# The third sweep (second batch norm's output, third layer norm) and the edge attention as one list of slots instead of loops one after the other

## Chip, cores and metric

The kernel runs on one core of a Trainium2 chip. The metric is the time of one execution on the device in microseconds (us); the median of three runs is given. TensorE multiplies matrices, VectorE (DVE in the rows) and ScalarE (ACT) work element by element, GpSimd (POOL) does so more slowly, and SyncE (SP) issues the transfers.

## The reference

`x` has 16 batches of 512 nodes with 128 features. Four graph blocks follow one another, each with a residual and a layer norm. The change touches the end of the third block and the whole fourth:

```
x = _layernorm(x + _L2_gnn_ref(x, adj, ...), axis=-1)      # out = batchnorm(out, g2, be2), added to x
x = _layernorm(x + _L3_gnn_ref(x, ..., adj, src, dst), axis=-1)
# _L3: 256 edges src -> dst, 4 heads of 32 features
Xq, Xv = H @ W_lin.T, H @ W_val.T
e  = einsum(leaky_relu(Xq[src] + Xq[dst], 0.2), a) + log(A0[src, dst] + EPS)
attn = softmax of e over the edges that share a src           # segment_max, exp, segment_sum
Y  = segment_sum(attn * Xv[dst], src);  return Y @ W_out.T
```

The second batch norm needs statistics over all 16 batches before it can be applied to any. After it, no batch depends on another.

## The kernel before

All of `X` stays in SBUF. The first 880 us compute the first two blocks and the graph product of the third; the change leaves their instructions and order alone. Then `phase_batchnorm` runs three sweeps over the batches. The second (L1864) multiplies by W2 and gathers statistics. Then `batch_norm` makes scale and shift (last write at L1935). The **third** sweep takes, per batch, the scaled output (`z`, ScalarE, L1894), its four transposes (L1875), the residual add (L1961) and four row statistics (L606) on VectorE. Per quad of four batches GpSimd makes layer-norm scale and shift (`norm_scales`, thirteen instructions L571 to L586, among them the inverse root L583), and ScalarE and VectorE apply them (L646, L625).

`phase_attention` begins when all engines have left that block. It has two loops. The **gather** loop splits X into a high and a low part (`aXH` on ScalarE, `aXL` on GpSimd, L72), multiplies both by the incidence matrix `GZ` (L2337, eight matmuls a batch), copies the result to `Z` (L2262), projects to scores and values (L2343, L2346, copied to `aUV` at L2146), takes the leaky ReLU `lr` (L2270) and the head scores (L2355). The softmax is done by scans along the sorted edges (L2237 to L2251), for three quads at once beside the last gather quad, and for the fourth after it. The attention weights `aT` of all batches are made in one go (L2292, L2293). Only then the **attend** loop starts: GpSimd weights the values (`va`, L2107), ScalarE and VectorE split them (`vah`, `val`), TensorE scatters them (L2386) and projects (L2376), VectorE adds (L2304) and takes statistics, GpSimd makes the norm of a quad, ScalarE applies it, SyncE stores.

Each engine runs its own list in order. A semaphore wait on an engine holds all that stands behind it. The loops are hardware loops (`Fori`) with their first and last pass written out (`peeled`). PSUM has eight banks of 128x512; in the gather loop banks 0 and 1 hold the gathered batch, 2 and 3 the projections, 4 the scores.

Of the kernel before, what the change touches and what calls it, by code (L numbers as in the profile page):

```python
# [552 lines left out]
SHIFT_LINKS = 6  # L553


def norm_scales(pool, sh, n, stats, work, mean, rstd, own, before, shift, free=None):

    a, b, c = (work[:, k, 0:n] for k in range(3))

    def const(k):
        return sh.const[:, k, 0:n]

    def link(k, ins):

        ins.then_inc(own, 1)
        pool.wait_ge(own, before + k)

    pool.tensor_tensor(a, stats[:, :, 1], stats[:, :, 4], ALU.add)  # L571
    pool.tensor_tensor(b, stats[:, :, 1], stats[:, :, 4], ALU.subtract)
    link(1, pool.tensor_tensor(c, stats[:, :, 2], stats[:, :, 5], ALU.add))
    pool.tensor_tensor(mean, a, const(sh.HALF), ALU.mult)
    pool.tensor_tensor(c, c, const(sh.PER_D), ALU.mult)
    link(2, pool.tensor_tensor(b, b, b, ALU.mult))
    link(3, pool.tensor_tensor(b, b, const(sh.QUARTER), ALU.mult))
    link(4, pool.tensor_tensor(b, b, c, ALU.add))
    link(5, pool.tensor_tensor(b, b, const(sh.EPS), ALU.add))
    if free is None:  # L580
        free = lambda: None
    pool.tensor_tensor(mean, mean, const(sh.MINUS), ALU.mult)
    link(6, pool.tensor_tensor(a, b, const(sh.ROOT), ALU.pow))  # L583
    free()
    pool.tensor_tensor(rstd, a, const(sh.ONE), ALU.mult)
    return pool.tensor_tensor(shift, mean, a, ALU.mult)  # L586


class NormBuffers:
# [3 lines left out]
    def __init__(self, sb, sem, sh):  # L593
        self.sh = sh
        self.rows = QB * sh.C
        self.stats = sb("nstats", [P, sh.NB * sh.C, 6])
        self.work = sb("nwork", [P, 3, self.rows])
        self.mean = sb("nmean", [P, self.rows])
        self.scale = sb("nscale", [P, self.rows])
        self.shift = sb("nshift", [P, self.rows])  # L600
        self.own = sem("norm_own")
        self.ready = sem("norm_ready")
# [10 lines left out]
    def scales(self, pool, g, own, before, free=None):  # L613

        return norm_scales(pool, self.sh, self.rows, self.stats[:, bass.ds(self.rows * g, self.rows), :],
                           self.work, self.mean[:, :], self.scale[:, :], own, before, self.shift[:, :], free)

    def apply_on_dve(self, dve, n, b, chunks=None, other=None):

        scale, shift = other or (self.scale, self.shift)  # L620
        C = self.sh.C
        for c in range(C) if chunks is None else chunks:
            k = b * C + c
            row = self.sh.X[:, c, bass.ds(n, 1), :]
            ins = dve.tensor_scalar(row, row, scale[:, k:k + 1], shift[:, k:k + 1], ALU.mult, ALU.add)  # L625
        return ins

    def finish_scales(self, pool, earlier):
        self.scales(pool, self.sh.NB // QB - 1, self.own, SHIFT_LINKS * earlier).then_inc(self.ready, 1)

    def finish(self, act, earlier, done, batches=range(QB)):
        act.wait_ge(self.ready, earlier + 1)
        for b in batches:
            self.apply(act, self.sh.NB - QB + b, b).then_inc(done, 1)

    def apply(self, act, n, b, chunks=None, other=None):

        scale, shift = other or (self.scale, self.shift)
        C = self.sh.C
        for c in range(C) if chunks is None else chunks:
            k = b * C + c
            row = self.sh.X[:, c, bass.ds(n, 1), :]
            ins = act.activation(row, row, ACT.Identity, bias=shift[:, k:k + 1], scale=scale[:, k:k + 1])  # L646
# [3 lines left out]
def take_over(nc, sh, later):  # L650
# [36 lines left out]
    sh.free_to = first  # L687
    sh.hidden = room("hidden", [P, NB, J, N], offset=first)
# [1134 lines left out]
def phase_batchnorm(nc, sh, d):  # L1823
# [8 lines left out]
    with ExitStack() as ctx:  # L1832
# [5 lines left out]
        O2 = nc.alloc_sbuf_tensor_at("O2", [P, NB, N], F32, offset=sh.outputs_at)  # L1838
        tmp = sh.A
        st2 = sb("st2", [P, 1, NB, 6])  # L1840
        bmv = sb("bmv", [P, J + 1, 2])
        bsc = sb("bsc", [P, J + 1])
        bsh = sb("bsh", [P, J + 1])
        norm = sh.norm
        names = ("own", "bmv_done", "bve", "brstd", "bn_done", "u_done", "o_mm", "o_out",
                 "ost_done", "z_done", "z_mm", "z_add", "stat_done", "norm_own", "rstd_done", "x_done", "xd_done")
# [3 lines left out]
        def xb(b):  # L1850
            return sh.X[:, :, bass.ds(b, 1), :].rearrange("p c o d -> p c (o d)")

        def by_chunk(ap):
            return ap.rearrange("p (c d) -> p c d", c=C)

        @block.tensor
        def _(pe):
# [10 lines left out]
            def third(i, last):  # L1868
                for b in range(QB):
                    n = QB * i + b  # L1870
                    pe.wait_ge(S["z_done"], n + 1)
                    wait(pe, S["z_add"], n - QB + 1)
                    for c in range(C):
                        cols = slice(c * P, (c + 1) * P)
                        ins = pe.transpose(sh.psum[:, b, cols], tmp[:, b, cols], sh.ident[:, :])  # L1875
                    ins.then_inc(S["z_mm"], 1)

            peeled(pe, NQ, second)
            peeled(pe, NQ, third)

        @block.scalar
        def _(act):
# [9 lines left out]
            def z(n, b):  # L1892
                wait(act, S["z_mm"], n - QB + 1)
                act.activation(tmp[:, b, :], O2[:, bass.ds(n, 1), :], ACT.Identity,  # L1894
                               bias=bsh[:, J:J + 1], scale=bsc[:, J:J + 1]).then_inc(S["z_done"], 1)

            def third(i, last):

                for b in range(QB):
                    if not last:  # L1900
                        z(QB * (i + 1) + b, b)
                    if not isinstance(i, int) or i > 0:
                        if b == 0:
                            act.wait_ge(S["rstd_done"], i)
                        norm.apply(act, QB * (i - 1) + b, b, range(C - 1)).then_inc(S["x_done"], 1)

            act.wait_ge(S["bn_done"], 1)
            peeled(act, NQ, second)
            act.wait_ge(S["bn_done"], 2)
            for b in range(QB):  # L1910
                z(b, b)
            peeled(act, NQ, third)

        @block.vector
        def _(dve):
# [37 lines left out]
            def third_stats(n):  # L1953
                dve.wait_ge(S["z_add"], n + 1)
                norm.take_stats(dve, n).then_inc(S["stat_done"], 1)

            def third(i, last):
                for b in range(QB):
                    n = QB * i + b
                    dve.wait_ge(S["z_mm"], n + 1)  # L1960
                    dve.tensor_tensor(xb(n), by_chunk(sh.psum[:, b, :]), xb(n), ALU.add).then_inc(S["z_add"], 1)  # L1961
                    if not isinstance(i, int) or n >= 1:
                        third_stats(n - 1)
                if not isinstance(i, int) or i > 0:
                    dve.wait_ge(S["rstd_done"], i)
                    for b in range(QB):
# [498 lines left out]
```

## Time and profile before

| | before |
|---|---|
| median of three runs | 1098.01 us (1094.91 to 1099.32) |
| the profiled execution | 1097.92 us, span 1096.1 us |
| third sweep | 921.0 to 957.5 us of the span |
| gather loop | 957.5 to 1030.5 us |
| softmax of the last quad, attention weights | 1030.5 to 1039.3 us |
| attend loop | 1039.3 to 1082.5 us |
| last norms and stores | 1082.5 to 1096.1 us |

The span is what the rows are timed in; the 1.8 us between it and the execution's own time lie outside the rows. A busy share says how long an engine had an instruction in work, not that it set the pace. A short idle time "<-" another engine says whose result ended the wait.

### The profile page before, as it was taken

How to read it: one execution, taken by the hardware profiler on the slowest of the kernel's cores; microseconds unless marked ns; L12 is line 12 of the kernel's file. 1: busy time of each engine (PE TensorE's matmuls, PEld its weight loads, DVE VectorE, ACT ScalarE, POOL GpSimd, SP SyncE). 2: the span in 40 equal slices, each digit the busy share in tenths (PEclk: the TensorE clock that was granted, in tenths of full speed). 3: DMA queues.
4: the chain of work that ended last, by engine and by line, in shares of the span. 5: the costliest groups of instructions: out<-in, count | busy, mean ns of one | idle time of the engine just before them, and what ended most of it. 6: DMA issues, size and time to landing. Idle time of an engine off the chain costs nothing. (4 is left out here: it accounts for less than half of the span.)

```text
span 1096.1 us, 14843 instructions
## 1 busy us (share of the span) xinstructions
PE 957.0 (87%) x5168; PEld 815.9 (74%) x5168; DVE 660.3 (60%) x1528; ACT 547.5 (50%) x1133; POOL 314.6 (29%) x373
## 2 busy tenths in 40 slices
PE   4999998899998999999999999799899886289583
PEld 2677997688997888998789889697689734166463
DVE  4843435334656736666655664788878857643665
ACT  2113233455645554554655554567677474742256
POOL 0001131222232223332223332324332300552256
PEclk9989999999999999999999999999999988589797
DMA  7003001000110000101010101210100000000004
GB/s 206 1 1 76 20 39 70 8 20 1 39 40 1 8 33 19 40 1 39 1 39 20 39 1 42 73 39 21 39 20 1 0 1 1 1 0 1 0 20 134
DMA packets 34137, 31.60 MB, mean 29 GB/s; under 512 B 8594, under 2 KB 28178, under 8 KB 34068
## 3 DMA queue, kind: packets, MB, share of 16 engines
q1 hardware_dynamic: 33108, 30.64, 9.1%
q8 instruction: 40, 0.66, 0.2%
q14 instruction: 29, 0.24, 0.1%
q10 hardware_dynamic: 960, 0.07, 0.1%
HBM read 22.83 MB, written 7.87 MB: 28 GB/s over the span
## 5 line engine op out<-in xcount | busy, mean ns | idle before, releaser
L1371 ACT ACTIVATE gates<-psum,gbias 128x256 f32<-128x256 f32 (+2 forms) x312 | 158.3, 565 | 56.3 <-PE psum L67 52.6
L65 PE MATMUL psum<-LS,WI 128*128 128x256 f32 (+2 forms) x312 | 104.8, 336 | 15.3 <-ACT gates L1371 11.6
L72 POOL TENSOR_TENSOR LS<-A,LS 128x512 fp32r<-128x512 f32 (+2 forms) x44 | 48.7, 1107 | 201.6 <-ACT LS L1356 201.6
L67 PE MATMUL psum<-LS,WI 128*128 128x256 f32 (+2 forms) x312 | 103.4, 331 | 0.0
L66 PE MATMUL psum<-LS,WI 128*128 128x256 f32 (+2 forms) x312 | 103.3, 331 | 0.0
L72 POOL TENSOR_TENSOR LS<-Hodd,LS 128x512 fp32r<-128x512 f32 (+2 forms) x44 | 48.7, 1107 | 160.2 <-ACT LS L1356 160.2
L65 PEld LDWEIGHTS psum<-LS,WI 128*128 128x128 f32 x312 | 60.0, 192 | 26.7 <-POOL LS L72 11.5
L65 PE MATMUL psum<-B2h,LT2h 128*128 128x256 f32 x256 | 72.8, 284 | 1.1 <-DVE X L1479 1.0
L72 DVE TENSOR_TENSOR yl<-psum,yh 128x512 fp32r<-128x512 f32 x58 | 39.7, 689 | 56.4 <-ACT yh L1313 41.4
L1378 ACT ACTIVATE tc<-cell 128x512 f32<-128x512 f32 (+2 forms) x88 | 45.2, 514 | 55.7 <-DVE cell L1659 39.9
L67 PE MATMUL psum<-B2h,LT2l 128*128 128x256 f32 x256 | 72.4, 283 | 0.0
L66 PE MATMUL psum<-B2l,LT2h 128*128 128x256 f32 x256 | 72.4, 283 | 0.0
L65 PE MATMUL psum<-Eh,yh 128*128 128x384 f32 x168 | 59.1, 352 | 12.0 <-DVE yl L72 12.0
L66 PEld LDWEIGHTS psum<-LS,WI 128*128 128x128 f32 x312 | 60.0, 192 | 5.1
L67 PEld LDWEIGHTS psum<-LS,WI 128*128 128x128 f32 x312 | 59.9, 192 | 4.2
L72 POOL TENSOR_TENSOR XSl<-X,XSh 128x512 fp32r<-128x512 f32 x32 | 42.6, 1333 | 69.5 <-ACT XSh L1308 69.3
L65 PE MATMUL psum<-LS,WH 128*128 128x256 f32 (+2 forms) x192 | 60.1, 313 | 0.0
L66 PE MATMUL psum<-LS,WH 128*128 128x256 f32 (+2 forms) x192 | 59.9, 312 | 0.0
L67 PE MATMUL psum<-LS,WH 128*128 128x256 f32 (+2 forms) x192 | 59.9, 312 | 0.0
L66 PE MATMUL psum<-El,yh 128*128 128x384 f32 x168 | 58.0, 345 | 0.0
L67 PE MATMUL psum<-Eh,yl 128*128 128x384 f32 x168 | 58.0, 345 | 0.0
L606 DVE BATCH_NORM_STATS2 nstats<-X 128x6 f32<-128x128 f32 (+1 forms) x256 | 55.1, 280 | 1.6 <-DVE X L2304 1.3
(388 smaller groups left out, 2718.5 us busy)
## 6 DMA issues: line engine op xcount, KB each, us to landing
WI<-lstm_weights SPq DMA_DIRECT2D x14, 512.0 KB, 3.5
WH<-lstm_weights SPq DMA_DIRECT2D x11, 512.0 KB, 4.5
X<-in_x SPq DMA_DIRECT2D x16, 256.0 KB, 5.0
out<-X SPq DMA_DIRECT2D x32, 128.0 KB, 1.9
lstm_weights<-WI SPq DMA_DIRECT2D x4, 512.0 KB, 2.6
lstm_weights<-WH SPq DMA_DIRECT2D x3, 512.0 KB, 2.6
A<-in_adj SPq DMA_DIRECT2D x1, 1024.0 KB, 6.2
z_A<-in_adj SPq DMA_DIRECT2D x1, 1024.0 KB, 5.1
```

The costliest lines, as they stand in the source:

```text
L65: pe.matmul(out, lhs[0], rhs[0], start=start, stop=False)
L66: pe.matmul(out, lhs[0], rhs[1], start=False, stop=False)
L67: return pe.matmul(out, lhs[1], rhs[0], start=False, stop=stop)
L72: return eng.tensor_tensor(out, full, high.bitcast(F32), ALU.subtract)
L606: return dve.bn_stats(self.stats[:, bass.ds(self.sh.C * n + c, 1), :], self.sh.X[:, c, bass.ds(n, 1), :])
L1371: act.activation(gates[:, gate, 0:n], sh.psum[:, gate, 0:n], ACT.Tanh if gate == G else ACT.Sigmoid, bias=gbias[:, p_ - 1, gate:gate + 1]) ...
L1378: act.activation(tcs[:, 0:n], cell[:, s % 2, 0:n], ACT.Tanh).then_inc(S["tanh_done"], 1)
```

## The change

The third sweep leaves `phase_batchnorm` and joins `phase_attention`. There every batch passes through all steps in a software pipeline, written as one flat list `order` that every engine walks through without a loop, taking its own items. Slot k holds, for different batches, these items: `z` and `T` (transpose, residual add) of batch k+5, `s3`/`v3`/`p3`/`sh3`/`ap3` (row statistics, variance, inverse root, shift and application of the third norm, in groups of one or two batches), `xs` (split) of batch k+2, `G` (gather) of batch k, `U` of k-1, `lr` and `W` of k-2, and from slot 9 on `S` (scatter) of batch k-9, `P` (projection) of k-10, and `R` (residual add), `s4` and the fourth norm of k-11 and older. The softmax of quad g stands in slots 4g+6 and 4g+7 (`sc`, `mx`, `df`, `ex`, `su`, `at`), so batches 0 to 3 can be attended to from slot 7.

The arithmetic of a norm moves: six short VectorE instructions and a shift replace twelve of the thirteen on GpSimd, which keeps the inverse root. `Z` is copied from PSUM by ScalarE instead of VectorE. The applications of the third norm are split 2+2, 1+3 or 3+1 chunks between VectorE and ScalarE by batch (`chunks3`), those of the fourth 2+2. The low part of the weighted values (`vl`) of batches 0 to 7 goes to GpSimd, of 8 to 15 to VectorE. PSUM: banks 0, 1 and 6 rotate among what VectorE reads (`T`, `at`, `P`), 2 to 5 among what ScalarE reads (`G`, `U`, `S`), 7 holds scores. The edge constants are made once instead of four times, in `phase_batchnorm` right behind the first `batch_norm`. The output goes out in 16 transfers of 256 KB, not 32 of 128 KB.

```diff
...
+    AHEAD, BEHIND = 5, 9
...
+        GROUPS3 = [(0, 1), (1, 2), (2, 3)] + [(b, min(b + 2, NB)) for b in range(3, NB, 2)]
+        GROUPS4 = [(0, 4), (4, 8), (8, 12), (12, 14), (14, 16)]
+        def first_part():
+            return [("z", 0), ("z", 1), ("T", 0), ("z", 2), ("s3", 0), ("v3", 0), ("p3", 0), ("T", 1), ("z", 3), ("s3", 1),
+                    ("v3", 1), ("p3", 1), ("T", 2), ("z", 4), ("sh3", 0), ("ap3", 0), ("xs", 0), ("s3", 2), ("v3", 2),
+                    ("sh3", 1), ("ap3", 1), ("xs", 1), ("p3", 2), ("T", 3), ("s3", 3)]
+        def slot(k):
+            t, m = k + AHEAD, k - BEHIND
+            g, part = divmod(k - 6, QB)
+            softmax = part if 0 <= g < NQ else None
+            ready = [i for i, (b0, b1) in enumerate(GROUPS3) if b1 == t and k > 1] + [2] * (k == 0) + [3] * (k == 1)
+            items = [("p3", i) for i in ready if i > 2]
+            if 0 <= m + 1 < NB:
+                items += [("vh", m + 1)]
+            if k == 0:
+                items += [("z", t)]
+            if t + 1 < NB:
+                items += [("z", t + 1)]
+            if 0 <= k - 2 < NB:
+                items += [("lr", k - 2)]
+            if softmax == 0:
+                items += [("sc", g), ("mx", g), ("df", g)]
+            if 0 <= m - 2 < NB:
+                items += [("R", m - 2)]
+            if 0 <= m + 1 < NB:
+                items += [("vl", m + 1)]
+            if 0 <= m - 2 < NB:
+                items += [("s4", m - 2)] + [("v4", i) for i, (b0, b1) in enumerate(GROUPS4) if b1 == m - 1]
+            if k < NB:
+                items += [("G", k)]
+            if k == 0:
+                items += [("T", t - 1)]
+            if t < NB:
+                items += [("T", t)]
+            if 4 <= k + 2 < NB:
+                items += [("xs", k + 2)]
+            if softmax == 0:
+                items += [("ex", g)]
+            if 0 <= k - 1 < NB:
+                items += [("U", k - 1)]
+            if softmax == 1:
+                items += [("at", g)]
+            items += [("sh3", i) for i in ready]
+            items += [("ap3", n) for n in ((2,), (3, 4))[k] if n < NB] if k < 2 else [("ap3", k + 3)] * (k + 3 < NB)
+            if k < 2:
+                items += [("xs", k + 2)]
+            if k == 0:
+                items += [("s3", t - 1), ("v3", 3)]
+            if t < NB:
+                items += [("s3", t)] + [("v3", i) for i, (b0, b1) in enumerate(GROUPS3) if b1 == t + 1]
+            if softmax == 0:
+                items += [("su", g)]
+            if 0 <= m < NB:
+                items += [("S", m)]
+            if 0 <= k - 2 < NB:
+                items += [("W", k - 2)]
+            if 0 <= m - 1 < NB:
+                items += [("P", m - 1)]
+            if 0 <= m + 2 < NB:
+                items += [("va", m + 2)]
+            items += [("p4", i) for i, (b0, b1) in enumerate(GROUPS4) if b1 == m - 1]
+            for i, (b0, b1) in enumerate(GROUPS4):
+                if b1 == m - 2:
+                    items += [("sh4", i)]
+                if b0 <= m - 2 - (b1 - b0) < b1:
+                    items += [("ap4", m - 2 - (b1 - b0))]
+            return items
+        order = first_part()
+        for k_ in range(NB + BEHIND + 5):
+            order += slot(k_)
+        for g_, (b0_, b1_) in enumerate(GROUPS4):
+            order += [item for item in [("sh4", g_)] + [("ap4", b) for b in range(b0_, b1_)] if item not in order]
...
+        def chunks3(n):
+            split = C // 2 if n < 3 else C - 1 if 5 < n < 11 else 1
+            return range(0, split), range(split, C)
+        def low_on_dve(n):
+            return n >= NB - BEHIND + 1
+        dve_ring, act_ring = {}, {}
+        for item_ in order:
+            if item_[0] in ("T", "at", "P"):
+                dve_ring[item_] = len(dve_ring)
+            elif item_[0] in ("G", "U", "S"):
+                act_ring[item_] = len(act_ring)
+        DVE_BANKS, ACT_BANKS = (0, 1, 6), (2, 3, 4, 5)
+        def dve_bank(item):
+            return sh.psum[:, DVE_BANKS[dve_ring[item] % len(DVE_BANKS)], :]
+        def act_bank(item):
+            return sh.psum[:, ACT_BANKS[act_ring[item] % len(ACT_BANKS)], :]
...
+            def variances(rows, work):
+                stats = norm.stats[:, rows, :]
+                a, b, c = (work[:, k, rows] for k in range(3))
+                dve.tensor_tensor(a, stats[:, :, 1], stats[:, :, 4], ALU.add)
+                dve.tensor_tensor(c, stats[:, :, 2], stats[:, :, 5], ALU.add)
+                link(dve.tensor_tensor(b, stats[:, :, 1], stats[:, :, 4], ALU.subtract))
+                link(dve.scalar_tensor_tensor(b, b, 0.25, b, ALU.mult, ALU.mult))
+                link(dve.scalar_tensor_tensor(b, c, 1.0 / D, b, ALU.mult, ALU.add))
+                return dve.tensor_scalar(b, b, EPS, None, ALU.add)
...
+            def roots(k, groups, g):
+                work, scale, _ = norms[k - 3]
+                rows = slice(C * groups[g][0], C * groups[g][1])
+                pool.wait_ge(S[f"var{k}"], g + 1)
+                pool.tensor_tensor(scale[:, rows], work[:, 1, rows], sh.const[:, sh.ROOT, 0:rows.stop - rows.start],
+                                   ALU.pow).then_inc(S[f"root{k}"], 1)
...
```

What TensorE had in its gather loop, the end of one pass (two batches: the last two of sixteen gather matmuls, the two batches' projections, their scores):

```order
L2337 MATMUL psum<-z_GZ,aXH 128x512
L2337 MATMUL psum<-z_GZ,aXL 128x512
L2343 MATMUL psum<-Z,z_aWT 128x256
L2346 MATMUL psum<-z_aWT,Z 128x128 x2
L2343 MATMUL psum<-Z,z_aWT 128x256
L2346 MATMUL psum<-z_aWT,Z 128x128 x2
L2355 MATMUL psum<-lr,wide 16x256 x2
```

TensorE in slot 10 of the change, from the end of `G` of batch 10 on (`T` of 15, `U` of 9, `S` of 1, `W` of 8, `P` of 0):

```order
L2097 MATMUL psum<-z_GZ,aXH 128x512
L2097 MATMUL psum<-z_GZ,aXL 128x512
L2088 MATMUL psum<-ident,A 128x128 x4
L2105 MATMUL psum<-aZ,z_aWT 128x256
L2108 MATMUL psum<-z_aWT,aZ 128x128 x2
L2136 MATMUL psum<-z_GsT,vah 128x512
L2136 MATMUL psum<-z_GsT,val 128x512
L2136 MATMUL psum<-z_GsT,vah 128x512
L2136 MATMUL psum<-z_GsT,val 128x512
L2116 MATMUL psum<-lr,wide 16x256
L2145 MATMUL psum<-z_aWT,aY 128x128 x4
```

The projections now follow the gather of another batch, and transposes and scatters that stood in loops of their own lie between them and the scores.

VectorE in the last gather pass before, with the softmax of three quads (768 wide) in it:

```order
L2262 COPY Z<-psum 128x512 x2
L2237 SCALAR_TENSOR_TENSOR s<-pf,sco 16x768
L2240 SCALAR_TENSOR_TENSOR s<-pr,s 16x768
L2270 SCALAR_TENSOR_TENSOR lr<-aUV 128x256 x2
L2244 TENSOR_TENSOR s<-sco,s 16x768
L2262 COPY Z<-psum 128x512 x2
L2248 SCALAR_TENSOR_TENSOR s<-kf,s 16x768
L2270 SCALAR_TENSOR_TENSOR lr<-aUV 128x256 x2
L2251 SCALAR_TENSOR_TENSOR sco<-pr,s 16x768
L2277 TENSOR_TENSOR sco<-psum,lg 16x256
```

VectorE in slot 6 of the change, with the softmax of the first quad, up to the `lr` of slot 7:

```order
L2320 TENSOR_TENSOR sco<-psum,lg 16x256
L2275 SCALAR_TENSOR_TENSOR s<-pf,sco 16x256
L2276 SCALAR_TENSOR_TENSOR s<-pr,s 16x256
L2324 TENSOR_TENSOR s<-sco,s 16x256
L2240 TENSOR_TENSOR X<-psum,X 128x4x128
L2263 SCALAR_TENSOR_TENSOR n3shift<-n3work,n3scale 128x8
L2295 TENSOR_SCALAR X<-X,n3scale,n3shift 128x128 x3
L566 BN_STATS nstats<-X 128x6 x4
L2280 SCALAR_TENSOR_TENSOR s<-kf,s 16x256
L2281 SCALAR_TENSOR_TENSOR sco<-pr,s 16x256
L2271 SCALAR_TENSOR_TENSOR lr<-aUV 128x256
```

Two copies to `Z` a pass are gone from this engine; the residual add, the application and the row statistics of the third norm have come in between the scans of one quad.

## Rows read from the trace of the kernel before

**Rows 1.** The profile page, its first line.

```profile
span 1096.1 us, 14843 instructions
```

**Rows 2.** Stages: busy us of PE, PEld, DVE, ACT, POOL; PEclk; DMA share, GB/s.

```profile
921.00:957.50 36.50, 14.32 (x64) 10.84 (x64) 26.16 (x92) 25.44 (x53) 16.04 (x40) 0.59 0.00 0
957.50:1030.50 73.00, 61.06 (x257) 43.93 (x257) 32.84 (x60) 27.81 (x50) 28.27 (x30) 0.91 0.00 1
1030.50:1039.30 8.80, 2.05 (x17) 1.63 (x16) 6.24 (x10) 1.08 (x3) 1.75 (x5) 0.56 0.00 0
1039.30:1082.50 43.20, 35.40 (x192) 29.16 (x192) 30.80 (x95) 27.04 (x67) 28.59 (x73) 0.93 0.17 50
1082.50:1096.10 13.60, 0.00 (x0) 0.00 (x0) 3.59 (x14) 6.70 (x18) 6.97 (x21) 0.51 0.55 154
```

**Rows 3.** Timeline of VectorE, third sweep: start, us, instructions, idle time before them.

```profile
922.96 1.47 DVE L1961 TENSOR_TENSOR X<-psum,X 128x512 f32<-128x512 f32 x2 [2.13 <-PE psum L1875]
...
925.12 0.67 DVE L1961 TENSOR_TENSOR X<-psum,X 128x512 f32<-128x512 f32 x1
925.72 0.86 DVE L606 BATCH_NORM_STATS2 nstats<-X 128x6 f32<-128x128 f32 x4
...
952.48 1.11 DVE L625 TENSOR_SCALAR X<-X,nscale,nshift 128x128 f32<-128x128 f32 x4
```

**Rows 4.** Chain that ended last, a gather pass: start, us, what.

```profile
987.06 3.92 PE psum L2337 x16
990.98 0.43 PE psum L2343 x2
991.41 0.45 PE psum L2346 x4
...
1002.10 0.60 PE psum L2355 x2
```

**Rows 5.** The same chain in the attend loop.

```profile
1048.15 1.19 PE psum L2386 x4
1049.34 0.91 PE psum L2376 x8
```

**Rows 6.** Timeline of TensorE, third sweep: one batch's transposes.

```profile
927.31 0.63 PE L1875 MATMUL psum<-ident,A 128*128 128x128 f32 x4 [0.34 <-ACT A L1894]
```

**Rows 7.** Timeline of VectorE, softmax of the last quad.

```profile
1034.95 0.68 DVE L2251 TENSOR_TENSOR_SCAN sco<-pr,s 16x256 f32<-16x256 f32 x1
1036.19 0.96 DVE L2292 RECIPROCAL inverse<-psum 128x128 f32<-128x128 f32 x1 [0.56 <-PE psum L2366]
```

**Rows 8.** Timeline of an earlier norm, its arithmetic on VectorE, root on GpSimd.

```profile
689.31 0.17 DVE L1508 TENSOR_TENSOR n1work<-nstats 128x8 f32<-128x8 f32 x1
...
690.17 0.68 DVE L1546 TENSOR_TENSOR B<-psum,RB 128x512 f32<-128x512 f32 x1
690.34 1.64 POOL L1774 TENSOR_TENSOR n1scale<-n1work,const 128x8 f32<-128x8 f32 x1 [3.83 <-DVE n1work L1513]
```

**Rows 9.** VectorE beside GpSimd in the gather loop: timelines of both.

```profile
984.92 0.75 DVE L2270 SCALAR_TENSOR_TENSOR lr<-aUV 128x256 f32 x1 [1.03 <-ACT aUV L2146]
...
984.12 1.27 POOL L72 TENSOR_TENSOR aXL<-X,aXH 128x512 fp32r<-128x512 f32 x1 [0.57 <-ACT aXH L2134]
```

**Rows 10.** One line's or tile's instructions: ns of one, min/median/max.

```profile
L2270 DVE SCALAR_TENSOR_TENSOR lr<-aUV x16: 417/426/1536, 967.0 to 1029.4; 128x256 f32<-128x256 f32 x8, 128x256 f32 x8
L625 DVE TENSOR_SCALAR X<-X,nscale,nshift x76: 331/340/1039, 449.4 to 953.3; 128x128 f32<-128x128 f32 x68, - x8
```

**Rows 11.** Groups of instructions by line: busy us, mean ns of one, idle before.

```profile
L72 DVE TENSOR_TENSOR LS<-gates,LS 128x256 fp32r<-128x256 f32 x24 | 22.4, 932 | 0.8
```

**Rows 12.** Attend loop: timelines of GpSimd and VectorE at one root.

```profile
1057.27 2.90 POOL L583 TENSOR_TENSOR nwork<-nwork,const 128x16 f32<-128x16 f32 x1
...
1058.90 0.41 DVE L72 TENSOR_TENSOR val<-va,vah 128x256 fp32r<-128x256 f32 x1
```

**Rows 13.** Timeline of ScalarE, the last norm's application.

```profile
1090.50 1.65 ACT L646 ACTIVATE X<-X,last_shift,last_scale 128x128 f32<-128x128 f32 x4 [2.95 <-POOL last_shift L586]
```

More of the change, by code:

```diff
@@ L550, in _ @@
             done(ins)
[L553 to L586, printed above, removed]
 class NormBuffers:
@@ L625, in apply_on_dve @@
             ins = dve.tensor_scalar(row, row, scale[:, k:k + 1], shift[:, k:k + 1], ALU.mult, ALU.add)
[L626 to L646, printed above, removed]
         return ins
@@ L687, in take_over @@
     sh.free_to = first
+    sh.consts_at = first - 4096
     sh.hidden = room("hidden", [P, NB, J, N], offset=first)
@@ L1951, in second, with edge_constants @@
                         second_stats(n - 1)
[L1953 to L1966, printed above, removed]
-                        ins = norm.apply_on_dve(dve, QB * (i - 1) + b, b, range(C - 1, C))
-                    ins.then_inc(S["xd_done"], 1)
+            def edge_constants():
+                dve.wait_ge(S["wide0"], 1)
+                dve.wait_ge(S["acol_in"], 16)
+                for h in range(NH):
+                    rows = slice(h * DH, (h + 1) * DH)
+                    dve.tensor_copy(wide[rows, R - NH + h:R - NH + h + 1], acol[rows, 0:1])
+                link(dve.tensor_tensor(ne[:, 1:NE], ss[0:R, 0, 1:NE], ss[0:R, 0, 0:NE - 1], ALU.not_equal))
+                dve.tensor_scalar(pf[:, 1:NE], ne[:, 1:NE], LOWEST, None, ALU.mult)
+                dve.tensor_scalar(kf[:, 1:NE], ne[:, 1:NE], -1.0, 1.0, ALU.mult, ALU.add)
+                dve.tensor_scalar(pr[:, 0:NE - 1], ne[:, 1:NE], LOWEST, None, ALU.mult)
+                dve.memset(pf[:, 0:1], LOWEST)
+                dve.memset(kf[:, 0:1], 0.0)
+                dve.memset(pr[:, NE - 1:NE], LOWEST)
             batch_norm(list(range(J)), 0)
+            edge_constants()
             peeled(dve, NQ, second)
@@ L2186, in _, with normalized @@
[L2186 to L2192 removed]
+            def normalized(n):
+                wait(act, S["pe_dve"], dve_ring["T", n - QB] + 1 if n >= QB else 0)
+                act.activation(tmp[:, n % QB, :], O2[:, n, :], ACT.Identity, bias=sh.bsh[:, sh.J:sh.J + 1],
+                               scale=sh.bsc[:, sh.J:sh.J + 1]).then_inc(S["z_done"], 1)
@@ L2275, in scores @@
-            def scores(g):
-                dve.wait_ge(S["sc_mm"], QB * g + QB)
-                dve.tensor_tensor(sco[:, bass.ds(g, 1), :].rearrange("p o e -> p (o e)"), sh.psum[0:R, 4, 0:NE],
-                                  lg[:, :], ALU.add).then_inc(S["sc_done"], 1)
-            def gather_quad(g, last):
-                for h in (0, 1):
-                    wait(dve, S["sc_mm"], QB * g + 2 * h)
-                    gather(g, h, last)
-                scores(g)
-            peeled(dve, NQ, gather_quad)
@@ L2310, in attend @@
-            def attend(i, last):
-                for b in range(QB):
-                    n = QB * i + b
-                    first = isinstance(i, int) and i == 0
-                    weighted_low(n, b)
-                    if not first or b >= 3:
-                        residual(n - 3, (b - 3) % QB)
-                        out_stats(n - 3)
-            peeled(dve, NQ, attend)
-            for n in range(NB - 3, NB):
-                residual(n, n % QB)
-                out_stats(n)
-            for n, made in ((NB - QB, NQ), (NB - QB + 1, NQ), (NB - 1, NQ + 1)):
-                dve.wait_ge(S["rstd_done"], made)
-                norm.apply_on_dve(dve, n, n % QB, other=last_norm).then_inc(S["xd_done"], 1)
@@ new lines, in rows_of, with shifts, leaky @@
+            def rows_of(groups, g):
+                return slice(C * groups[g][0], C * groups[g][1])
+            def shifts(k, g, rows):
+                work, scale, shift = norms[k - 3]
+                dve.wait_ge(S[f"root{k}"], g + 1)
+                dve.scalar_tensor_tensor(shift[:, rows], work[:, 0, rows], -0.5, scale[:, rows], ALU.mult, ALU.mult)\
+                    .then_inc(S[f"shift{k}"], 1)
+            def leaky(n):
+                dve.wait_ge(S["act_free"], act_ring["U", n] + 1)
+                if n >= QB:
+                    dve.wait_ge(S["sc_mm"], n - QB + 1)
+                u = UV[:, n, 0:NE]
+                dve.scalar_tensor_tensor(lr[:, n % QB, :], u, 0.2, u, ALU.mult, ALU.max).then_inc(S["lr_done"], 1)
```

600 lines of the change are left out of this document (281 added, 319 removed).

## Prediction

> **What bounds the kernel now.** The page gives the span, 1096.1 us [rows 1]. I read the part behind the second batch norm stage by stage, since the share of the whole says nothing of it. From 921.0 to the end it lasts 175.1 us in five stages [rows 2]. The reader is to see that no engine is full in any but one of them. In the third sweep TensorE is busy 14.3 of 36.5 us at 0.59 of its clock, VectorE 26.2, and both wait for the norm's scales from GpSimd. In the gather loop TensorE is the bound, 61.1 of 73.0 us, and VectorE has 40 us to spare. The softmax of the last quad and the weights of all batches are a bare chain, 8.8 us. In the attend loop TensorE (35.4) and VectorE (30.8) share 43.2 us. The last 13.6 us are one norm after another on GpSimd, then the stores. Summed over the five rows TensorE has 112.8 us of work (part of it at the low clock) and VectorE 99.6. So a perfect overlap could save at most some 60 us, and what it does save depends on which engine is longest in each stretch of the new list.
>
> **The sum.** I go through the list by stretches and take in each the engine with most work, at durations of the old trace.
>
> *Start.* The first residual add began at 922.96 [rows 3]. The list has a block change ahead of it, which cost some 0.3: 923.3.
>
> *To the end of slot 10, by VectorE.* Sixteen residual adds at 0.60 from start to start and sixteen statistics of four at 0.86 [rows 3]: 23.4. Ten groups of variance, six instructions from 689.31 to 690.17, 0.86, and one shift at 0.17 [rows 8]: 10.3, with the waits in them 10.5. Of the third norm 27 chunks are applied here by then, 1.11 for four [rows 3]: 7.6. Nine `lr` at 0.43 [rows 10]: 3.9. Two quads of softmax: four scans at 0.7 [rows 7] and two 256-wide passes at 0.41 [rows 12] are 3.6 each; weights of the first quad 0.6 (the reciprocal is 0.96 for 128 columns [rows 7] and 32 are left, so between 0.24 and 0.96 with the product; I take the middle). Sum 53.2. TensorE has in the same slots eleven gathers at 1.96, ten projections at 0.88, nine scores at 0.6 [rows 4], twelve transposes at 0.63 [rows 6], two scatters at 1.19 and a projection at 0.91 [rows 5]: 46.7. It cannot begin before batch 0 has been added, normed, applied and split, some 8 us after 923.3; with 3.5 for the low clock (below) that ends at 981.5. So VectorE sets the end, narrowly: 923.3 + 53.2 = 976.5.
>
> *What VectorE waits for in there.* First, crossings: in slot 6 and slot 10 it has some 7.5 us of work where TensorE has 4 to 6, and the weights `at` need the scans done on VectorE, then TensorE, then VectorE again. What stands behind the waiting `at` is the shift and application of the third norm, for which `xs` and `G` of two slots later wait; the two slots of lead cover it. I take 3 us, bounds 0 and 8 (half a slot each time). Second, GpSimd beside it. `lr` started at 984.92 and took 0.75, while `aXL` ran on GpSimd from 984.12 to 985.39; alone it takes 0.42 [rows 9, 10]. It ended 0.28 after the GpSimd instruction, as if it had waited for it. Over sixteen `lr` the median is 0.426 and the longest 1.536 [rows 10], and for the applications 0.340 and 1.039. The row nearest at the upper end is the earlier `LS` subtraction of the same 256 columns, mean 0.932 [rows 11]: half a microsecond of waiting in each. I take 4 us in all, since the median `lr` waits for nothing; bounds 0 and 22 (43 exposed instructions or groups at 0.51). End of slot 10: 983.5.
>
> The Trainium skill, page "SBUF — State Buffer", section "Who interferes with whom", has for this that a VectorE instruction with two SBUF inputs and a GpSimd instruction that reads SBUF exclude each other for the whole instruction. The trace agrees at `lr`, and does not at the inverse root: `val`, two SBUF inputs, took 0.41 at 1058.90 in the middle of a root that ran from 1057.27 to 1060.17 [rows 12]. By the page the roots, moved beside the whole list, would count as blockers too; by the row they don't. What full blocking would give is the rival below.
>
> *Slots 11 to 15, by TensorE.* Gather 1.96, projection 0.88, scores 0.6, scatter 1.19, projection 0.91, so 5.55 a slot, and 0.4 twice for the weights: 28.5, to 1012.0. VectorE has some 20 us here, so it is hidden and can catch up what it lags. `Z` on ScalarE instead of VectorE is hidden as well: ScalarE's list holds about 3.6 us a slot in the first stretch and no more here; if that cover were gone it would cost 0.6 a slot.
>
> *Slots 16 to 25, by VectorE again.* Ten adds with statistics at 1.46 and ten times two chunks of the fourth norm at 0.28: 20.2. Eight `val` at 0.41: 3.3. Two `lr`: 0.9. Three groups' variances: 3.2. The last quad's softmax and weights: 4.2. Sum 31.8, to 1043.8. TensorE has only scatter and projection here, 2.1 a slot against 3.2, and the 2.9 of a four-batch root runs on GpSimd beside it.
>
> *Tail.* Last add and statistics 1.46, variance 0.86, root of eight columns 1.64 and shift 0.17 [rows 8], two batches applied by halves on two engines, on ScalarE 1.65 for four chunks [rows 13], and from the last application to the end what it is today, 1096.1 less 1092.15 [rows 1, 13]: 3.95. Together 9.7, to 1053.5. The last store is one of 256 KB instead of four of 128 KB for two batches; I count no difference, at most tenths.
>
> *Handoffs.* The new list changes partner more often than the loops did, but has no loop registers to count. Bounds 0 and 10 over 30 slots; I take 2.8. End of span 1056.3.
>
> Against its own 1096.1 that is 39.8 less, and with the 1.8 us that the profiled execution has outside its span, 1058.1. The profiled execution (1097.92) and the median (1098.01) are the same, so **1058** is the forecast, 0.964 of before. Edge constants cost nothing: VectorE makes them while the first, slow-clock products of the second sweep run.
>
> **Where the 40 us come from.** The third sweep's 36.5 us mostly go, as its work now lies beside gathers; the bare 8.8 goes; of the attend loop and tail 56.8 become 41.5; the gather stretch stays about as long. It does not shrink, because VectorE and TensorE are near each other there.
>
> **Rivals.**
>
> *Low clock.* TensorE's granted clock was 0.91 over the gather loop and 0.59 and 0.56 in the stages where it mostly idled [rows 2]. 0.91 over 73 us are some 13 us at 1.2 GHz instead of 2.4, which cost about 6.6; I took half. In slots 16 to 25 TensorE is busy 2.1 of 3.2 us. The attend loop kept 0.93 at 35.4 of 43.2 busy, so I expect the high level; if it fell, 4.2 a slot would pass VectorE's 3.2 and cost 10, another 7 us early on 3.5: 1072. Chance 0.12.
>
> *Port waits at mid height.* If the scans, variances and applications all meet `aXL` and the new `vl` on GpSimd, 22 instead of 4 in the first eleven slots, less what slots 11 to 15 absorb: 1066 to 1084. Chance 0.13.
>
> *Port waits all along: slower than before.* GpSimd now has 3.7 us in each of slots 7 to 13, where the gather loop had 1.3 a batch. VectorE has some 135 exposed pieces (16 `lr`, 20 passes of softmax, 8 `val`, 30 variances and shifts, 61 calls of application). At the 0.51 of the `LS` row that is 69 us, 65 more than I count, 8 of them hidden in the middle: 1115. It decides at 0.32 each (44 us). Against it: the median `lr` and the median application show nothing. Chance 0.04.
>
> *No change.* The slots do not overlap: every slot lasts as long as the fullest, 5.55 by 26 slots, and 18 us of start and tail make 162 of today's 175; with waits in the softmax slots 1086 to 1098. For it speaks only that each engine's list is in order. Chance 0.04.
>
> *Better.* No port waits, no crossings, no handoffs: 9.8 less, and 2 or 3 from weights and low clock, 1046. Chance 0.12.
>
> **How the numbers follow.** The forecast, 1050 to 1067, has 0.55. The range 1046 to 1076 takes in the better case, the low clock and the lower half of the port waits. A measurement tells about 0.5% (5.5 us) from no change. Faster by more than that has all of the forecast, better, low clock and middle port cases and half of the no-change case: 0.94. Within it 0.02, slower 0.04.
>
> **What would show it.** Right: the stretch behind the second batch norm is about 135 us; TensorE's clock stays above 0.9 in it after the first 20 us; the first scatter starts near 975, while gathers go on; VectorE is over 90% busy in slots 0 to 10 and TensorE over 90% in 11 to 15; 10 us lie between the last projection's add and the end; ScalarE loads its exponential table once. Wrong: `lr`, scans or applications with means twice their least; long idle times of TensorE "<- DVE lr" in the softmax slots; GpSimd near full, so that `aXL` comes late; the clock at 0.5 in the last third.

## The result, and the profile after

The changed kernel took 1063.32 us (1061.85 to 1063.46, 4 runs) beside 1098.35 (1094.91 to 1099.32) of the kernel before on the same chip: a ratio of 0.968, interval 0.966 to 0.971, 35 us faster. The forecast was 1058, the range 1046 to 1076. One of the four executions of the kernel called "attend late" below took 1372.26 us at a granted clock of 0.65 and is left out of its ratio. The page, in its first line and its busy times:

```profile
span 1061.5 us, 14487 instructions
...
PE 947.9 (89%) x5168; PEld 810.5 (76%) x5168; DVE 678.0 (64%) x1653; ACT 540.3 (51%) x1114; POOL 300.6 (28%) x279
```

The part behind the second batch norm, cut at the events of the prediction: first split done, slot 11 on TensorE, slot 16 on TensorE, last projections (columns as in [rows 2]):

```profile
921.70:932.90 11.20, 3.68 (x16) 3.28 (x16) 8.21 (x35) 5.14 (x8) 3.29 (x3) 0.65 0.00 1
932.90:990.80 57.90, 48.54 (x235) 36.43 (x235) 49.66 (x153) 38.66 (x75) 31.40 (x28) 0.93 0.00 1
990.80:1019.10 28.30, 27.70 (x151) 20.95 (x151) 22.56 (x67) 17.00 (x38) 19.20 (x26) 1.00 0.00 1
1019.10:1048.60 29.50, 23.26 (x132) 19.11 (x130) 26.89 (x95) 15.76 (x38) 10.38 (x14) 0.88 0.27 77
1048.60:1061.50 12.90, 0.19 (x2) 0.00 (x1) 8.37 (x37) 4.58 (x12) 3.33 (x2) 0.55 0.53 151
```

The 175.1 us of [rows 2] are now 139.8. The reader is to see that TensorE is full only in the third row (27.7 of 28.3) and VectorE nearly so in the fourth. In the second, where the forecast had VectorE over 90% busy, it is busy 49.7 of 57.9, and 86% is also an overstatement: part of that is instructions held up. The chain that ended last, around slot 9 to 11 (start, us, what):

```profile
972.84 1.34 DVE lr L2271
974.18 0.60 DVE X L2240
975.27 0.95 DVE X L2295 x3
976.22 0.79 DVE nstats L566 x4
978.05 1.76 POOL n3scale L2349
979.84 0.69 DVE n3shift L2263
...
984.88 1.20 DVE n3work L2252
...
993.82 0.69 DVE sco L2281
994.55 0.29 PE psum L2127 x2
994.84 1.14 PE psum L2136 x4
```

It runs through VectorE as forecast, but with `lr` at 1.34 us instead of 0.43, one pass of a variance at 1.20 instead of 0.17, and a detour over GpSimd's root.

### The profile page after: what moved, and what is told of

It is laid out like the page before. It is cut to its first block and busy times, and to the rows that moved or that the text cites. A ratio compares the mean times of both kernels' runs of the same rounds, so it can differ in the third digit from the quotient of the medians.

```text
span 1061.5 us, 14487 instructions
## 1 busy us (share of the span) xinstructions
PE 947.9 (89%) x5168; PEld 810.5 (76%) x5168; DVE 678.0 (64%) x1653; ACT 540.3 (51%) x1114; POOL 300.6 (28%) x279
## 5 line engine op out<-in xcount | busy, mean ns | idle before, releaser
L566 DVE BATCH_NORM_STATS2 nstats<-X 128x6 f32<-128x128 f32 x256 | 54.1, 277 | 0.4
```

What stands on the lines that cost most here:

```text
L566: return dve.bn_stats(self.stats[:, bass.ds(self.sh.C * n + c, 1), :], self.sh.X[:, c, bass.ds(n, 1), :])
```

## The measure used below

Medians of this kernel spread by a few us, and the run below shows that most of that can lie ahead of the change. I therefore compare profiled executions by the **stretch**, from the start of the last write of the batch norm's shift (`bsh`) to the end of the span. For the changed kernel these rows give 1061.5 − 921.58 = 139.9:

```profile
921.58 0.16 DVE L1850 TENSOR_TENSOR bsh<-z_par,bsh 128x1 f32<-128x1 f32 x1
```

**The same kernel again.** No edit. 

> The changed kernel once more, nothing edited, as a measure of how well times repeat. The code up to the end of the second batch norm is the same in all runs, and the profiled executions reached it at times between 915.5 and 924.6 us. If the spread of the medians (a few us) comes from that part alone, the stretch behind it is 139.9 us again within 0.3, and the start of it lies anywhere between 915 and 925. If the stretch itself varies by more than 1 us, the differences of 1 to 3 us between the runs above say nothing.

Its span is 1058.6 us, and in its timeline:

```profile
918.74 0.16 DVE L1850 TENSOR_TENSOR bsh<-z_par,bsh 128x1 f32<-128x1 f32 x1
```

The stretch is 1058.6 − 918.74 = 139.9 again (139.92 and 139.86), while its start moved by 2.8 us; the median was 1065.24 (1060.48 to 1065.85), ratio 0.972 (0.970 to 0.974). So, as far as two profiles of one kernel can tell, a difference of 1 us between stretches means something, and one of 3 us between medians hardly. The table has one profile for each kernel; each ratio is against executions of the kernel before on the same chip.

| kernel | stretch, us | against changed | ratio to before (interval) |
|---|---|---|---|
| changed | 139.9 | | 0.968 (0.966–0.971) |
| one ring of banks | 139.8 | −0.1 | 0.969 (0.967–0.971) |
| no aXL | 132.9 | −7.0 | 0.963 (0.961–0.966) |
| no aXL, sums forward | 131.7 | −8.2 | 0.964 (0.961–0.967) |
| sums forward | 138.8 | −1.2 | 0.969 (0.967–0.972) |
| attend late | 149.5 | +9.6 | 0.978 (0.975–0.981) |
| norm on GpSimd | 157.8 | +17.9 | 0.985 (0.983–0.988) |
| third norm to ScalarE | 137.1 | −2.8 | 0.967 (0.965–0.969) |
| fourth norm to ScalarE | 139.1 | −0.8 | 0.969 (0.967–0.971) |
| both to ScalarE | 136.1 | −3.9 | 0.967 (0.965–0.970) |
| both, sums forward | 137.2 | −2.8 | 0.967 (0.965–0.970) |
| fourth norm, last four | 141.2 | +1.3 | 0.972 (0.969–0.974) |

## Experiments on why slot 10 ended late

The theory from the chain above, called the port theory below: VectorE's small instructions wait for GpSimd's `aXL`. The rival: it is the root's latency and the crossings of the softmax. VectorE and GpSimd in the changed kernel, timelines (start, us, instruction, idle time before it):

```profile
950.17 1.26 DVE L2263 SCALAR_TENSOR_TENSOR n3shift<-n3work,n3scale 128x8 f32<-128x8 f32 x1 [2.62 <-POOL n3scale L2349]
...
980.56 1.28 DVE L2295 TENSOR_SCALAR X<-X,n3scale,n3shift 128x128 f32<-128x128 f32 x1
...
984.80 1.27 DVE L2252 TENSOR_TENSOR n3work<-nstats 128x8 f32<-128x8 f32 x1
...
987.68 0.68 DVE L2275 TENSOR_TENSOR_SCAN s<-pf,sco 16x256 f32<-16x256 f32 x1
```

```profile
948.51 1.63 POOL L2349 TENSOR_TENSOR n3scale<-n3work,const 128x8 f32<-128x8 f32 x1
950.11 1.30 POOL L72 TENSOR_TENSOR aXL<-X,aXH 128x512 fp32r<-128x512 f32 x1
...
980.46 1.30 POOL L72 TENSOR_TENSOR aXL<-X,aXH 128x512 fp32r<-128x512 f32 x1
...
984.70 1.34 POOL L72 TENSOR_TENSOR aXL<-X,aXH 128x512 fp32r<-128x512 f32 x1 [0.97 <-ACT aXH L2176]
...
987.07 1.75 POOL L2349 TENSOR_TENSOR n3scale<-n3work,const 128x8 f32<-128x8 f32 x1 [0.31 <-DVE n3work L2255]
```

Three VectorE instructions that start within 0.1 us of an `aXL` end within 0.1 us of it. The first pair is no accident: `aXL` follows the root in GpSimd's list, and the shift follows the root on VectorE, so the root's end releases both. And the scan at 987.68, two SBUF inputs, takes its usual 0.68 in the middle of a root.

**No aXL.** 

> The changed kernel, with the low half of the split (aXL) of batches 2 to 15 left out: GpSimd computes a power of six columns of constants in its place, about as long (1.3 us) and with the same semaphore, but without reading wide rows of SBUF. The gathers of these batches therefore add a stale low half. Port-wait theory (VectorE's small instructions wait for aXL, some 11 us in slots 0 to 10): the whole becomes 7 to 10 us shorter than the changed kernel's 1063.3, 1053 to 1056; the longest shift, variance and lr fall from 1.2 or 1.3 us to below 0.6. Rival (the slots are late by crossings and the latency of the root on GpSimd, the port hardly counts): 1060 to 1063, and the waits on n3scale stay. A third outcome is that a power of constants blocks VectorE as well: then the longest ones stay at 1.2.

```diff
+small = sb("small_pow", [P, NB, 6])
...
 pool.wait_ge(S["xh_done"], n + 1)
+if n >= 2:
+    pool.tensor_tensor(small[:, n, :], sh.const[:, sh.EPS, 0:6], sh.const[:, sh.ROOT, 0:6], ALU.pow)\
+        .then_inc(S["xl_done"], 1)
+    continue
```

Groups of instructions by line, of the changed kernel and then of this one (busy us, mean ns of one):

```profile
L2271 DVE SCALAR_TENSOR_TENSOR lr<-aUV 128x256 f32<-128x256 f32 x16 | 9.4, 590 | 3.5 <-ACT aUV L2180 3.4
L2295 DVE TENSOR_SCALAR X<-X,n3scale,n3shift 128x128 f32<-128x128 f32 x29 | 10.7, 410 | 0.3
L2263 DVE SCALAR_TENSOR_TENSOR n3shift<-n3work,n3scale 128x8 f32<-128x8 f32 x6 | 4.1, 690 | 4.2 <-POOL n3scale L2349 4.2
```

```profile
L2272 DVE SCALAR_TENSOR_TENSOR lr<-aUV 128x256 f32<-128x256 f32 x16 | 7.1, 446 | 4.1 <-ACT aUV L2181 4.0
L2296 DVE TENSOR_SCALAR X<-X,n3scale,n3shift 128x128 f32<-128x128 f32 x29 | 8.9, 349 | 0.3
L2264 DVE SCALAR_TENSOR_TENSOR n3shift<-n3work,n3scale 128x8 f32<-128x8 f32 x6 | 2.0, 340 | 6.4 <-POOL n3scale L2350 6.4
```

```profile
L2369 POOL TENSOR_TENSOR small_pow<-const x14: 1312/1322/1567, 937.0 to 996.1; 128x6 f32<-128x6 f32 x14
```

GpSimd is occupied as long as before (1.32 us a batch), yet the stretch lost 7.0 us, and the second quad's sums (end of slot 10 on VectorE) came 66.5 us behind the batch norm instead of 72.9. That is the lower edge of what the port theory asked. VectorE's busy time up to those sums, the changed kernel first (columns as in [rows 2]):

```profile
921.58:994.50 72.92, 55.37 (x266) 42.24 (x266) 61.48 (x200) 47.23 (x91) 36.85 (x34) 0.89 0.00 1
```

```profile
918.13:984.61 66.48, 53.55 (x266) 40.99 (x266) 52.91 (x200) 47.16 (x91) 37.76 (x34) 0.91 0.00 1
```

The same 200 instructions take 8.6 us less, and 6.4 of it reach the sums. An `lr` that starts inside one of the powers takes its usual time (VectorE, then GpSimd):

```profile
964.42 0.42 DVE L2272 SCALAR_TENSOR_TENSOR lr<-aUV 128x256 f32<-128x256 f32 x1
```

```profile
963.94 1.57 POOL L2369 TENSOR_TENSOR small_pow<-const 128x6 f32<-128x6 f32 x1 [2.52 <-ACT aXH L2177]
```

The granted clock differs between the two kernels as well (below), but only from 53 us behind the batch norm on; the first quad's sums end before that, at 46.3 instead of 51.2 us, so 5.0 of the 7.0 us owe nothing to the clock. Of the rival one half stands: the wait for `n3scale` stayed, and grew from 4.2 to 6.4. What is left of long instructions (a shift of 0.70 us, an `lr` of 0.63, both above the 0.6 expected) lies beside the shorter `val`, which I kept (VectorE, then GpSimd):

```profile
970.52 0.70 DVE L2264 SCALAR_TENSOR_TENSOR n3shift<-n3work,n3scale 128x8 f32<-128x8 f32 x1 [0.93 <-POOL n3scale L2350]
```

```profile
970.46 0.74 POOL L72 TENSOR_TENSOR val<-va,vah 128x256 fp32r<-128x256 f32 x1
```

**Sums forward.** 

> The changed kernel with the softmax's sums moved forward in its slot: the exponential stands directly behind the gather (before the split of x), and the two scans of the sums stand ahead of the fourth norm's variances, the third norm's shift, application and statistics. TensorE idled 2.3, 0.6 and 3.3 us for those scans before it could turn the weights. If these crossings count (the prediction took 3 us, up to 8): the idle times shrink to a third and the stretch behind the second batch norm, 139.9 us, loses 2 to 5, 1058 to 1061 in all. Rival (VectorE is full in slots 0 to 10 and is only made to wait for ScalarE's exponential ahead of work that it could do): no change up to slot 10, or 1 to 2 us more, and a gain of at most 2 us after slot 18.

```diff
+            if softmax == 0:
+                items += [("ex", g)]
...
             if t < NB:
                 items += [("T", t)]
+            if softmax == 0:
+                items += [("su", g)]
+            items += held
             if 4 <= k + 2 < NB:
                 items += [("xs", k + 2)]
-            if softmax == 0:
-                items += [("ex", g)]
...
-            if softmax == 0:
-                items += [("su", g)]
```

(`held` is the slot's `v4`; the old place of `su` was behind `s3`.) TensorE's waits from 925 us on (us, times, longest), of the changed kernel and of this one:

```profile
PE psum L2097 <- POOL aXL L72: 8.0, 3, 6.2
PE psum L2127 <- DVE sco L2281: 6.2, 3, 3.3
PE psum L2116 <- DVE lr L2271: 4.5, 4, 1.6
```

```profile
PE psum L2119 <- DVE lr L2274: 5.9, 5, 1.9
PE psum L2130 <- DVE sco L2284: 3.0, 2, 2.4
```

TensorE's wait for the sums halved, its wait for `lr` behind them grew by 1.4, and the stretch lost 1.2 us: between theory and rival, nearer the rival. The last quad's sums end 1.9 us earlier (107.8 instead of 109.7 us behind the batch norm), and 0.7 of it is lost again behind them. Together with the missing `aXL`: 

> The sums forward, and the low half of the split (aXL) of batches 2 to 15 left out as before, with a power of constants in its place on GpSimd. The run without aXL ended the sums of the second quad (slot 10) 66.5 us behind the second batch norm instead of 72.9; the prediction had 62.7. If what is left are crossings: the second quad's sums now end near 63 and the stretch takes 129 to 131 us (132.9 without the sums forward). If they are not: 132 to 134.

The second quad's sums ended at 63.1, where the prediction had 62.8, but some 2 us of that are only their earlier place in the slot; the stretch was 131.7, between its two ranges. So this move of the sums is worth 1.2 us with `aXL` and 1.2 without, and the waits for `aXL` 7. What other crossings cost, no run shows.

**Whose work sets the time.** 

> The changed kernel with the third norm applied to one chunk of four of every batch by VectorE, and three by ScalarE (the change gives VectorE two of batches 0 to 2 and three of batches 6 to 10). 13 chunks less at 0.28 are 3.6 us less on VectorE before the end of slot 10, 13 more at 0.41 are 5.4 on ScalarE, which is busy 38.7 of 57.9 us there. If VectorE's own work sets the end of slot 10: 3 to 4 us shorter behind the second batch norm, 1059 to 1060. Rival (those chunks fill time in which VectorE would wait for GpSimd or TensorE anyway, or ScalarE's application makes the split late): no change or 1 to 3 us slower.

```diff
-split = C // 2 if n < 3 else C - 1 if 5 < n < 11 else 1
+split = 1
```

13 chunks fewer on VectorE, −2.8 us of 3.6 at most, just short of the 3 to 4 asked. The second quad's sums end 2.5 us earlier (70.4 instead of 72.9): VectorE's work does set slots 0 to 10. For slots 16 to 25: 

> The changed kernel with the fourth norm of batches 0 to 13 applied to one chunk by VectorE and three by ScalarE instead of two and two, and with the low half of the weights (val) of batches 8 to 13 on GpSimd instead of VectorE. VectorE is busy 26.9 of 29.5 us in slots 16 to 25; 14 chunks at 0.28 and six val at 0.41 take 6.4 us off it. If VectorE sets that stretch, TensorE's 2.1 us a slot becomes the next bound and 3 to 6 us go, 1057 to 1060. Rival (the clock: with TensorE faster through its small work, or the scores' scans and the val on GpSimd at 0.73 as a longer chain): no change, 1062 to 1066.

```diff
+def chunks4(n):
+    split = 1 if n < 14 else C // 2
+    return range(0, split), range(split, C)
...
-return n >= NB - BEHIND + 1
+return n >= 14
```

Only −0.8, the rival's side. VectorE's busy time over the stretch fell by 3.9 us (115.8 to 111.9), not by 6.4, and its waits for projections rose from 2.3 to 4.0. TensorE's timeline in the last projection of this run:

```profile
1046.46 1.16 PE L2149 MATMUL psum<-z_aWT,aY 128*128 128x128 f32 x8 [1.75 <-ACT aY L2184]
```

The changed kernel has 1.09 us of idle time there. ScalarE's eviction of `Y` now comes later; that its additional chunks delay it is the likely reason, not one that I isolated. Both edits: 

> Both of the edits above together. They are in different stretches of the list, so by the theory that VectorE sets both stretches their gains add: 6 to 9 us, 1054 to 1057. If the first one is hidden: as the second alone.

−3.9, the sum of the two (−3.6), though less than the 6 to 9 asked. With the sums forward as well: 

> The sums forward, and with it the two edits to who applies the norms (third: one chunk of four on VectorE; fourth: one of four up to batch 13, val of batches 8 to 13 on GpSimd), which took 3.9 us off the stretch behind the second batch norm. If they add: 133 to 135 us of stretch instead of 139.9, 1056 to 1059 in all, 0.963 of before. If the sums forward are worth nothing: 136.

137.2, 1.1 worse than without: the gains do not add. The last quad's sums still end 0.4 us earlier than without the move (106.8 instead of 107.2), but the last projection ends 19.0 us behind them instead of 17.5. So the loss lies in the slots behind the last softmax; its cause stays open. The version with both edits has the shortest stretch of those that compute everything, 136.1; its ratio, 0.967, cannot be told from the changed kernel's.

## Experiments on where the gain comes from

**Attend late.** 

> The changed kernel with the attend part of a batch 17 slots behind its gather instead of 9, so that no scatter lies beside a gather; eight slots more at the end that hold nothing but attend work. Theory (the gain comes from overlap of two stages with different limits): VectorE has 52 us less the attend work of five batches in slots 0 to 10 unchanged, slots 11 to 15 lose 2.1 us each on TensorE (10 us) and get near VectorE's load, and eight batches more at 3.2 us come behind: 28 us less 10 or so, so 10 to 18 us slower, 1073 to 1081. Rival (most of the 35 us came from the third sweep beside the gathers, the attend overlap is worth nothing as VectorE is full anyway): 1062 to 1067.

```diff
-AHEAD, BEHIND = 5, 9
+AHEAD, BEHIND = 5, 17
...
-return n >= NB - BEHIND + 1
+return n >= 8
```

+9.6, just below the 10 to 18 asked: the overlap of scatters with gathers is worth that much of the 35. In the windows the five slots that TensorE filled now have it waiting:

```profile
990.10:1018.40 28.30, 23.25 (x108) 16.26 (x107) 17.08 (x39) 14.28 (x31) 12.52 (x17) 0.94 0.00 1
```

**Norm on GpSimd.** 

> The changed kernel with the arithmetic of both norms back on GpSimd, twelve instructions and the power as before the change; VectorE computes no variances and no shifts. VectorE loses 15 groups of 0.86 to 1.3 us and their port waits, some 16 to 18 us of its 115.7, GpSimd gains 15 times about 2.5 us. If VectorE's load is what sets the time and GpSimd has room: 5 to 10 us faster, 1053 to 1058. If the latency of the norm and GpSimd's load decide (aXL late behind the norm): 5 to 15 us slower, 1068 to 1078; TensorE would then wait longer for aXL. I take slower as likelier, 0.6.

```diff
-    variances(rows_of(GROUPS3, n), norms[0][0]).then_inc(S["var3"], 1)
...
-    shifts(3, n, rows_of(GROUPS3, n))
...
+link(pool.tensor_tensor(b, b, b, ALU.mult))
...
+link(pool.tensor_tensor(a, b, const(sh.ROOT), ALU.pow))
+pool.tensor_tensor(rstd, a, const(sh.ONE), ALU.mult)
+pool.tensor_tensor(shift[:, rows], mean, a, ALU.mult).then_inc(S[f"shift{k}"], 1)
```

Its waits, and the sum row of its windows over the stretch:

```profile
DVE X L2295 <- POOL n3shift L2368: 24.2, 8, 6.3
ACT X L2196 <- POOL n3shift L2368: 21.7, 8, 3.7
```

```profile
sum 157.80, PE 109.85 PEld 83.83 DVE 98.57 ACT 81.72 POOL 104.51; mean PE 21.97 PEld 16.77 DVE 19.71 ACT 16.34 POOL 20.90
```

+17.9, above my 5 to 15. VectorE has 17 us less to do (98.6 against 115.7) and stands still 24 us for the shift. In this list half of the gain hangs on the norm's arithmetic being on VectorE; with it on GpSimd the flat list brings 175.4 − 157.8 = 17.6 us. What the third sweep beside the gathers is worth by itself, or `Z` on ScalarE, no run shows.

**One ring of banks.** 

> The changed kernel with the seven PSUM banks as one ring for all results in TensorE's order, instead of three banks for what VectorE reads and four for what ScalarE reads. Whoever holds that the split by reader is worth something expects TensorE to wait for a bank of the slower reader, 3 to 10 us more (1066 to 1073). My own: a bank comes round after 1.3 slots and its reader is done well before, so no change, 1062 to 1065.

```diff
-DVE_BANKS, ACT_BANKS = (0, 1, 6), (2, 3, 4, 5)
+BANKS = 7
...
+return sh.psum[:, place[item] % BANKS, :]
...
+old = ring[place[item] - BANKS]
```

−0.1: the split of the banks by reader is worth nothing in this list.

**Fourth norm, last four as one group.** 

> The changed kernel with the fourth norm of batches 12 to 15 as one group instead of two of two. Behind the last statistics stand then a power of 16 columns (2.9 to 3.2 us instead of 1.64) and the application of four batches instead of two (ScalarE 1.65 us more), 3.1 us longer; in the slots before it VectorE saves one group's variance and shift and the application of batches 12 and 13, some 2 us, of which a part counts. Theory (the tail is a bare chain, as the prediction's 9.7 us has it): 1 to 3 us slower in all and the tail from the last add to the end 12 us. Rival: no difference.

```diff
-GROUPS4 = [(0, 4), (4, 8), (8, 12), (12, 14), (14, 16)]
+GROUPS4 = [(0, 4), (4, 8), (8, 12), (12, 16)]
```

```profile
1047.19 2.93 POOL L2349 TENSOR_TENSOR n4scale<-n4work,const 128x16 f32<-128x16 f32 x1 [7.49 <-DVE n4work L2255]
1050.36 3.19 ACT L2196 ACTIVATE X<-X,n4shift,n4scale 128x128 f32<-128x128 f32 x8 [6.75 <-DVE n4shift L2263]
```

The tail, last add to end, is 12.2 instead of 9.05, as expected, and 1.3 of it reach the stretch. The tail is a bare chain.

## Why the prediction was right, and where its sum was off

The forecast of the stretch was 1056.3 − 920.7 = 135.6; it is 139.9. By its own terms:

- *Start*: first add 924.3 instead of 923.3. Most of it is that the batch norm before it ended 0.9 later, which also varies between runs.
- *To the end of slot 10*: TensorE begins slot 11 at 69.2 us of the stretch, VectorE ends its sums at 72.9; forecast 62.8. The term mis-sized is the port waits: taken at 4, bounds 0 and 22, they are 8.6 in VectorE's busy time up to here, of which 6.4 reach the sums. VectorE's work itself was nearly right: 53.2 in the sum, 52.9 busy without `aXL`. The row chosen for the waits, the median `lr`, was the wrong one. Six of the sixteen `lr` of the old gather loop were held, at 0.75 to 1.54 us, one in nearly every pass, and a median does not show that; here the list itself also releases the shift and `aXL` by one event. Crossings: 3 taken; moving the sums forward gave 1.2, which is not all that crossings can cost. A term that was missing is VectorE's wait for the root, 4.2 us before `n3shift`. So the rival "port waits at mid height" (0.13) had the mechanism here, at some 40% of its 22 us; the whole still came out 3 us below its 1066. One comparison of the prediction is wrong by its own numbers: it lets VectorE set the end "narrowly" at 976.5, though its sum for TensorE ended at 981.5. Only the 7 us of waits put VectorE behind TensorE, and without any the time could fall by 2 us here, not 7, before TensorE set it. Without `aXL` TensorE began slot 11 at 62.0 us, near the 60.8 of that sum.
- *Slots 11 to 15 by TensorE*: 28.3 us against 28.5, TensorE 98% busy. Right, and the 3.7 us by which VectorE lagged were made up here, as the prediction said it could.
- *Slots 16 to 25 by VectorE*: 33.4 against 31.8. VectorE is 91% busy, but the run with less work on it gained only 0.8 us: while its work shrank, its waits for projections grew. That a ring binds there (VectorE waits for TensorE, TensorE for ScalarE's copies and VectorE's `val`) fits these waits, but no run isolates it.
- *Tail*: 9.05 against 9.7.
- *Handoffs*: 2.8 taken; nothing is left that needs them. Net, with 69.2 − 62.8 = 6.4 for the begin of slot 11 on TensorE: 6.4 − 0.2 + 1.6 − 0.7 − 2.8 = 4.3. That the 10.1 us missed at the end of slot 10 shrank to 4.3 is foreseen for 3.7 of them, the catching up in slots 11 to 15; that handoffs and tail were taken 3.5 too high is luck.
- *Signs*: the first scatter came at 983.4 instead of 975, in step with the late slot 10. VectorE was 86% busy in slots 0 to 10, not over 90%. The exponential table was loaded once.
- *Low clock*: the sign "above 0.9 after the first 20 us" was missed (0.88 in the fourth window). Two spells came that were not in the sum, one behind 2.27 and 1.08 us of idle TensorE in slots 6 and 7, one that began inside the 3.31 us of idle in front of the last quad's weights (windows, then the timeline of the second):

```profile
974.80:978.20 3.40, 3.40 (x9) 2.67 (x9) 3.23 (x16) 1.12 (x2) 0.93 (x3) 0.50 0.02 5
1029.40:1031.30 1.90, 0.00 (x0) 0.00 (x0) 1.76 (x6) 0.00 (x0) 1.26 (x1) 0.50 0.00 0
1031.30:1036.20 4.90, 4.89 (x17) 4.28 (x18) 4.38 (x15) 1.67 (x4) 3.98 (x7) 0.50 0.21 59
```

```profile
1031.31 0.39 PE L2127 MATMUL psum<-ident,sco 16*128 16x16 f32 x2 [3.31 <-DVE sco L2281]
...
1033.51 1.91 PE L2145 MATMUL psum<-z_aWT,aY 128*128 128x128 f32 x8
...
1036.60 1.05 PE L2145 MATMUL psum<-z_aWT,aY 128*128 128x128 f32 x8
```

The same eight projections take 1.91 us at the 1.2 GHz level and 1.05 at 2.4. Two scatters with projections cost 3.4 and 2.3 us instead of 1.8, so 2.1 us, which may be part of the missing 1.6. The first spell lies where the chain runs through VectorE. The kernels without `aXL` and with the third norm on ScalarE do not have it (1.00 there), and their second one lasts 3.4 us instead of 6.8; with the sums forward it is also 3.4. So up to 2 us of the 7.0 without `aXL`, and part of the 2.8 and of the 1.2, may be clock.

The rule weighed in the prediction, of the Trainium skill ("SBUF — State Buffer", "Who interferes with whom"), fits the rows of the changed kernel for wide instructions: `lr`, variances and shifts wait for the whole `aXL`, and so does an application (980.56, 1.28 us), which has one wide input; the section names `tensor_scalar` among those that can take both port pairs. Against a root it does not hold: the scan at 987.68 lost nothing, and neither did the `lr` at 964.42 inside a power of six columns in the run without `aXL`.

## What to carry to other kernels

Overlapping two loops with different limits pays what the fuller engine allows in each stretch, so sum the engines by stretch, then ask which instructions of one list are released by the same event as a wide GpSimd instruction: a 0.16 us instruction behind such an event costs 1.3. A median hides a hold-up that meets fewer than half of the instructions: look at the longest ones and at what ran beside them. Where small norm arithmetic sits between two uses of the same engine, keep it on that engine, though it is the bound: taking 17 us off VectorE cost 18 here.

## What I had not expected of the hardware

A power of six columns occupies GpSimd for 1.32 us and leaves VectorE alone, a split of 512 columns for 1.30 and holds it up; how busy GpSimd is says nothing of what it blocks. And the same code up to the end of the second batch norm took from 915.5 to 924.6 us in thirteen profiled executions, while the 140 us behind it repeated within 0.1 in the two of the same kernel.
